# Three of four block sums of x by accumulating transfers, with their casts and splits in new places

## The reference

```
q = cond @ Wq.T + bq                       # one row per batch, 16 heads of 32
k = x @ Wk.T + bk
v = x @ Wv.T + bv
scores = einsum over the 32 values of a head of q / sqrt(32) and k
attn = clip(scores, 0, 1)                  # one number per row and head
context = attn * v                         # per head
out = x + context @ Wo.T + bo
```

## Time and profile before

| what | value |
|---|---|
| three timed runs | 187.72, 187.91, 188.17 us (median 187.91) |
| the profiled execution's own time | 188.1 us |
| its span, first to last instruction | 186.3 us |
| PE busy | 182.5 us, 98% of the span |
| DVE busy | 168.8 us, 91% |
| ACT busy | 115.4 us, 62% |
| POOL busy | 14.7 us, 8% |
| granted PE clock | 1.00 of full speed (2.4 GHz) throughout |
| transfers | 28.09 MB, 151 GB/s over the span |
| the chain of work that ended last | PE 96%, DMA 2% |

### The profile page before, as it was taken

How to read it: one execution, slowest core, us unless ns; L and a number is a source line. 1 busy time by engine, 2 the same in 40 slices (tenths; PEclk the granted TensorE clock), 3 DMA queues, 4 the chain that set the end, 5 groups by cost and what they waited for, 6 DMA issues and landing times.

```text
span 186.3 us, 2377 instructions
## 1 busy us (share of the span) xinstructions
PE 182.5 (98%) x811; PEld 149.1 (80%) x811; DVE 168.8 (91%) x186; ACT 115.4 (62%) x158; POOL 14.7 (8%) x21
## 2 busy tenths in 40 slices
PE   8999999999999999999999999999999999999993
PEld 2788878878878888888888888888888888888883
DVE  0799998999999999999999999998997899799763
ACT  3589873977469685745388574862686574775200
POOL 8000000000000010021000010111000010111000
PEclk9999999999999999999999999999999999999999
DMA  5999910006600006289992006299920007289795
GB/s 218 340 388 425 408 62 2 0 0 193 253 10 0 0 0 116 113 126 230 246 421 106 0 0 116 113 134 296 246 115 0 0 0 116 113 127 279 157 369 194
DMA packets 8075, 28.09 MB, mean 151 GB/s; under 512 B 897, under 2 KB 1281, under 8 KB 7937
## 3 DMA queue, kind: packets, MB, share of 16 engines
q1 hardware_dynamic: 6336, 21.67, 30.4%
q0 software_dynamic: 1728, 6.29, 19.9%
HBM read 19.57 MB, written 8.39 MB: 150 GB/s over the span
## 4 chain that ended last, share of the span: by engine, by line
PE 96%; DMA 2%; ACT 0%; DVE 0%; issue 0%
PE bank_y L337 9%; PE bank_y L341 9%; PE bank_y L339 9%; PE bank_x L337 8%; PE bank_x L341 8%; PE bank_x L339 8%; PE bank_z L341 6%; PE bank_z L339 6%; PE bank_z L337 6%; PE bank_x L415 4%; PE score_bank L397 4%; PE score_bank L396 4%; PE bank_z L415 3%; PE bank_x L433 2%; DMA work<-first_t 2%; PE bank_y L415 1%
## 5 line engine op out<-in xcount | busy, mean ns | idle before, releaser
L574 ACT CAST form_hi<-work 128x1024 fp32r<-128x1024 f32 x28 | 29.0, 1051 | 24.6 <-PE score_bank L397 11.5
L850 DVE TENSOR_TENSOR form_lo<-work,form_hi 128x1024 fp32r<-128x1024 f32 (+1 forms) x38 | 40.2, 1077 | 4.3 <-ACT form_hi L574 4.3
L609 ACT ACTIVATE work<-bank_y,const 128x512 f32<-128x512 f32 x30 | 19.9, 688 | 9.6 <-PE bank_y L341 9.6
L831 POOL DMA_DIRECT2D work<-x_t x12 | 10.5, 875 | 150.7 <-DVE work L885 144.4
L337 PE MATMUL bank_x<-form_hi,wo_hi 128*128 128x512 f32 x52 | 20.3, 390 | 0.0
L339 PE MATMUL bank_x<-form_lo,wo_hi 128*128 128x512 f32 x52 | 20.2, 389 | 0.0
L341 PE MATMUL bank_x<-form_hi,wo_lo 128*128 128x512 f32 x52 | 20.2, 389 | 0.0
L609 ACT ACTIVATE work<-bank_x,const 128x512 f32<-128x512 f32 x24 | 16.0, 686 | 5.3 <-PE bank_x L341 5.3
L874 DVE SCALAR_TENSOR_TENSOR work<-relu,work 128x1024 f32<-128x1024 f32 x16 | 19.1, 1217 | 0.0
L337 PE MATMUL bank_y<-form_hi,wv_hi 128*128 128x512 f32 x48 | 18.8, 391 | 0.0
L341 PE MATMUL bank_y<-form_hi,wv_lo 128*128 128x512 f32 x48 | 18.7, 389 | 0.0
(11 more groups left out here) (153 smaller groups left out, 393.9 us busy)
## 6 DMA issues: line engine op xcount, KB each, us to landing
x_raw<-x_t SPq DMA_DIRECT2D x16, 512.0 KB, 7.0
out_t<-work SPq DMA_DIRECT2D x14, 512.0 KB, 3.3
work<-x_t POOLq DMA_DIRECT2D x12, 512.0 KB, 5.6
work<-first_t SPq DMA_DIRECT2D x2, 512.0 KB, 3.8
work<-wq_t SPq DMA_DIRECT2D x2, 512.0 KB, 8.7
work<-wk_t SPq DMA_DIRECT2D x2, 512.0 KB, 11.2
work<-wo_t SPq DMA_DIRECT2D x1, 1024.0 KB, 13.6
out_t<-work SPq DMA_DIRECT2D x3, 256.0 KB, 2.0
```

Source lines behind the costliest of these rows:

```text
L574: nc.scalar.copy(flat(form_hi, kind), raw(kind, phase)).then_inc(hi_ready[kind], 1)
L609: nc.scalar.activation(result_set(phase)[:, q, j * ROWS:(j + 1) * ROWS], of[:, j, :], ACT.Identity, bias=bias[:, tile:tile + 1], scale=sca ...
L831: pool.dma_start(output_set(s)[:, q, :], x_t[s, q], accum_op=ALU.add).then_inc(residual_added[q], 16)
L850: return nc.vector.tensor_tensor(to, of, hi.bitcast(F32), ALU.subtract)
```

## The change

The four x sums of each super-chunk were four DVE instructions. Now only T1 is one. T3, T2 and T4 are made by transfers that POOL issues and that add a block of x from HBM onto what lies in SBUF: T3 adds Q22 onto Q12 in `x_raw`, T2 adds Q22 onto T1 in `x_sum`, T4 adds Q21 onto T2 in `x_sum`. A transfer of T2 waits until T1 is both cast and split, one of T4 until T2 is both cast and split. In POOL's list these nine transfers stand between the twelve residual transfers. `next_x` waits for T1 of the super-chunk before instead of the split of T4.

Then the lists of ACT and DVE are written in another order. `hi(T4, 1)` now stands directly ahead of `copy_u2(1)`; `hi(T4, 3)` and `hi(T4, 5)` now stand behind `copy_u2(3)` and `copy_u2(5)`, where they stood ahead. The splits `lo(T4, ...)` move accordingly. In the opening, several copies and casts of weights change places.

```diff
@@ sync
             def next_x(s):
                 if s > 1:
-                    sp.wait_ge(lo_ready[T4], made(T4, VALUES_AT[s - 1]))
+                    sp.wait_ge(x_t1_ready, s - 1)
@@ scalar, order of the steps (cut)
             first_hi(T3, Q12)
-            wv_sum_part(S4, 2)
+            first_values(Q11, banks[0], 0)
             first_hi(B22, Q22)
-            first_values(Q11, banks[0], 0)
-            first_values(Q21, banks[1], 2)
...
             first_values(Q22, banks[0], 6)
             hi(B11, 1)
             hi(B21, 1)
             round_scores(0, 0)
-            hi(T4, 1)
-            wo_sum_part(S4, 3)
+            hi(T2, 1)
             hi(T3, 1)
             round_scores(0, 1)
             hi(B22, 1)
             copy_b11(1)
             relu_scores(0, 0)
             relu_scores(0, 1)
+            hi(T4, 1)
             copy_u2(1)
             hi(B11, 2)
...
-            hi(T4, 3)
             hi(B22, 3)
             hi(B11, 4)
             round_scores(2, 0)
+            hi(B21, 4)
             copy_u2(3)
-            hi(B21, 4)
+            hi(T4, 3)
             hi(T1, 4)
+            relu_scores(2, 0)
             copy_u3(3)
@@ gpsimd
-            for s in range(3):
-                at = OUTPUTS_AT[s]
-                add_residual(s, Q11, out11_added, at)
-                add_residual(s, Q22, out22_added, at)
-                add_residual(s, Q21, out21_copied, 2 * at)
-                add_residual(s, Q12, out12_added, at)
+            def x_t3(s):
+                pool.wait_ge(x_t1_ready, s)
+                pool.dma_start(x_raw[:, Q12, :], x_t[s, Q22], accum_op=ALU.add).then_inc(x_t3_ready, 16)
+
+            def x_t2(s):
+                pool.wait_ge(hi_ready[T1], made(T1, VALUES_AT[s]))
+                pool.wait_ge(lo_ready[T1], made(T1, VALUES_AT[s]))
+                pool.dma_start(x_sum[:, :], x_t[s, Q22], accum_op=ALU.add).then_inc(x_t2_ready, 16)
+
+            def x_t4(s):
+                pool.wait_ge(hi_ready[T2], made(T2, VALUES_AT[s]))
+                pool.wait_ge(lo_ready[T2], made(T2, VALUES_AT[s]))
+                pool.dma_start(x_sum[:, :], x_t[s, Q21], accum_op=ALU.add).then_inc(x_t4_ready, 16)
+
+            x_t3(1)
+            x_t2(1)
+            x_t4(1)
+            for s in range(2):
+                residual_11(s)
+                x_t3(s + 2)
+                x_t2(s + 2)
+                residual_22(s)
+                x_t4(s + 2)
+                residual_21(s)
+                residual_12(s)
@@ vector, the three sums go
-            def x_t3(phase):
-            def x_t2(phase):
-            def x_t4(phase):
@@ vector, order of the steps (cut)
             lo(B11, 1)
             lo(B21, 1)
             split_scores(0, 0)
-            lo(T4, 1)
+            wo_sum_part(S3, 2)
+            lo(T2, 1)
             lo(T3, 1)
+            lo(B22, 1)
             split_scores(0, 1)
-            lo(B22, 1)
             context(0, Q11)
             context(0, Q21)
-            wo_sum_part(S3, 2)
             add_out11(1)
             context(0, Q12)
+            lo(T4, 1)
             context(0, Q22)
             lo(B11, 2)
```

More of the change, by code:

```diff
@@ L801, in _ @@
             copy_u2(5)
+            hi(T4, 5)
             hi(T1, 6)
@@ L838, in _, with residual_11, residual_22, residual_21 @@
             nc.gpsimd.tensor_copy(select[:, :], const[:, C_SELECT:C_SELECT + P]).then_inc(select_ready, 1)
-            for s in range(3):
-                at = OUTPUTS_AT[s]
-                add_residual(s, Q11, out11_added, at)
-                add_residual(s, Q22, out22_added, at)
-                add_residual(s, Q21, out21_copied, 2 * at)
-                add_residual(s, Q12, out12_added, at)
+            def residual_11(s):
+                add_residual(s, Q11, out11_added, OUTPUTS_AT[s])
+            def residual_22(s):
+                add_residual(s, Q22, out22_added, OUTPUTS_AT[s])
+            def residual_21(s):
+                add_residual(s, Q21, out21_copied, 2 * OUTPUTS_AT[s])
+            def residual_12(s):
+                add_residual(s, Q12, out12_added, OUTPUTS_AT[s])
+            def x_t3(s):
[20 more added lines that the diff above has]
+                residual_12(s)
+            residual_11(2)
+            residual_22(2)
+            residual_21(2)
+            residual_12(2)
         @block.vector
@@ L934, in x_t1 @@
                 dve.wait_ge(x_loaded[Q12], loads(Q12, s))
+                if s > 1:
+                    dve.wait_ge(hi_ready[T4], made(T4, VALUES_AT[s - 1]))
                 nc.vector.tensor_tensor(x_sum[:, :], x_raw[:, Q11, :], x_raw[:, Q12, :], ALU.add).then_inc(x_t1_ready, 1)
-            def x_t3(phase):
[L939 to L942, removed]
-            def x_t2(phase):
[L946 to L949, removed]
-                nc.vector.tensor_tensor(x_sum[:, :], x_sum[:, :], x_raw[:, Q22, :], ALU.add).then_inc(x_t2_ready, 1)
-            def x_t4(phase):
-                s = PHASES[phase][1]
-                dve.wait_ge(hi_ready[T2], made(T2, phase))
-                dve.wait_ge(x_t2_ready, s)
-                dve.wait_ge(x_loaded[Q21], loads(Q21, s))
-                nc.vector.tensor_tensor(x_sum[:, :], x_sum[:, :], x_raw[:, Q21, :], ALU.add).then_inc(x_t4_ready, 1)
             def add_x(q):
@@ L1191, in _ @@
             add_out12(1)
+            lo(T3, 2)
+            split_scores(1, 1)
             context_t4(2)
-            split_scores(1, 1)
-            lo(T3, 2)
             add_out11(2)
+            x_t1(3)
             lo(T4, 2)
             lo(B22, 2)
-            x_t1(3)
             lo(B21, 3)
-            split_a(1)
-            x_t3(3)
+            context(1, Q11)
             lo(T1, 3)
-            x_t2(3)
+            context(1, Q12)
             add_out22(2)
-            lo(T2, 3)
-            lo(T3, 3)
-            context(1, Q11)
-            x_t4(3)
-            context(1, Q12)
-            add_out12(2)
-            lo(T4, 3)
-            add_out11(3)
-            lo(B22, 3)
-            split_scores(2, 0)
-            lo(B11, 4)
-            context_t1(4)
             context(1, Q21)
             context(1, Q22)
+            lo(T3, 3)
+            lo(T2, 3)
+            add_out12(2)
+            lo(B22, 3)
+            add_out11(3)
+            lo(B11, 4)
+            split_scores(2, 0)
+            context_t1(4)
             lo(B21, 4)
+            context_t3(4)
+            lo(T4, 3)
             lo(T1, 4)
@@ L1223, in _ @@
             lo(T2, 4)
-            context_t3(4)
+            context_t4(4)
             lo(B11, 5)
-            context_t4(4)
             x_t1(5)
+            context(2, Q11)
+            lo(T4, 4)
             add_out12(3)
-            lo(T4, 4)
+            lo(T3, 4)
             split_scores(2, 1)
-            lo(T3, 4)
+            lo(B22, 4)
             add_out11(4)
-            lo(B22, 4)
             lo(B21, 5)
-            x_t3(5)
-            context(2, Q11)
+            context(2, Q21)
             context(2, Q12)
+            context(2, Q22)
             lo(T1, 5)
-            x_t2(5)
             add_out22(4)
@@ L1242, in _ @@
             lo(T2, 5)
-            x_t4(5)
-            context(2, Q21)
-            context(2, Q22)
-            lo(T4, 5)
             add_out12(4)
```

64 lines of the change are left out of this document (31 added, 33 removed).

## The result

The change makes the kernel slower: 190.72 us median of four runs (190.30, 190.42, 191.02, 192.12) against 187.90 of four, a ratio of 1.0162 with a 95% interval from 1.0106 to 1.0218. The forecast was 188.8, in a range up to 190.1. The profiled execution took 190.42 us with a span of 188.6, 2.3 us more than before.

A forecast was written before the change was run, and what follows sets the result against it. PE's never-empty matmul queue was taken as the bound, so only new PE waits count: one wait of 0.85 us on the profiled 188.1 gives 188.95, and with the runs' median 0.2 lower, 188.8 us; range 187.7 to 190.1.

The forecast's parts named there:

- What bounds the kernel: From 5 to 183 us PE's matmul queue never runs dry; waits sum to 0.2 us, any new wait adds in full.
- the lighter DVE would give nothing: Some 11 us of DVE sums removed beside PE's work: worth 0; the rival that it gives something, 187.6 at best, had 0.03.
- PE's rows before 50 us moved by more than 0.2 us: One of the signs named in advance that would show the forecast wrong.
- Super-chunk 1: T4 issued at 41.4, landing at 48.7 after 7.3 us, delays U2's copy; PE starts T3 of phase 1 0.85 us late.
- The prediction's other estimate, 6.7: Landing of T4 in super-chunk 1 if transfer and loads took turns: 5.5 plus 1.2 us; 0.25 us of wait.
- Super-chunks 2 and 3: Phases 3 and 5: T4's transfer issued at 83.3 lands by 91.9, cast and split by 94.1; cost 0.
- 4 us of slack: Super-chunk 2: T4 cast and split by 94.1 at the latest, against PE's need at 98.14.
- The bound of 8.6: Longest landing of the twelve residual transfers before, beside a load and two stores; taken as upper limit for T4's landing.
- PE's need of T4 at 98.14: Phase 3: the time PE needs T4, taken as the deadline for its cast and split.
- another wait, in phases 2 to 5, by a residual or by T2 that lands late: Rival: such a wait costs 0.5 to 1.5 us, time 188.4 to 189.4 if it comes alone; chance 0.06.

The follow-up runs named there:

- e4: Changed kernel with only the old wait put back: the next super-chunk's loads wait for T4's split; 187.95 us, ratio 0.9996.
- e9: The kernel of e4 run again for its profile at full clock; 187.64 us, ratio 0.9986.
- e13: The kernel of e9 once more, timed in more rounds (12 runs); 187.57 us, ratio 0.9984.
- e12: Changed kernel with the moves of e3 and e7 together; 189.55 us, ratio 1.0083.
- e11: Changed kernel with the old wait on T4's split put back for the loads of super-chunk 3 alone; 188.35 us, ratio 1.0030.
- e2: Changed kernel with the sum T2 back on DVE, T3 and T4 still transfers; 188.49 us, ratio 1.0044.
- e7: Changed kernel with ACT's casts of T4 behind the copies of U3 in phases 3 and 5, DVE's splits one place later; 189.37 us, ratio 1.0072.
- e3: Changed kernel with T4's cast in phase 1 behind the copy of U2 and the score rounding, its split behind the score split; 191.53 us, ratio 1.0156.
- e10: Changed kernel with the old wait on T4's split put back for the loads of super-chunk 2 alone; 188.72 us, ratio 1.0037.
- e1: Changed kernel with the sum T4 back on DVE, T3 and T2 still transfers; 188.54 us, ratio 1.0039.

## Why the prediction was wrong

**What bounds the kernel: right.** PE has no slack, and every pause went into the span in full: 3.1 us of pauses, less 0.8 of a shorter opening, is 2.3 us. That the lighter DVE would give nothing was right too, within what can be told; e4, e9 and e13, which have all of the change but the loads' wait, lie 0.04% to 0.16% below the kernel before. One of the prediction's own signs of being wrong, PE's rows before 50 us moved by more than 0.2 us, came with the 0.8 of the opening; executions of the kernel before have spans from 185.6 to 186.6, so that much of it may be scatter.

**Super-chunk 1: right in place and cause; the size is close in part by luck.** T4's transfer was issued at 41.02 (forecast 41.4) and took 6.6 us (forecast 7.3), the cast started at 47.66 (48.7), and PE paused 0.68 us (0.85). Two errors worked against each other. The landing was 0.7 us shorter than forecast, but the issue came only 8.3 us ahead of PE's T3 (49.35), where the forecast had 8.8 (41.4 and 50.16): PE came 0.8 us earlier, the issue only 0.4. Beside the same loads it took 6.6 in e12, 6.8 in e11, 6.9 in e2 and e7, 7.1 in e3; without them 5.3 to 5.5 in e9, e10 and e13. So a meeting with three loads costs 1.1 to 1.8 us. The prediction's other estimate, 6.7, which is 5.5 alone and the 1.2 of one load, is nearer to this than the 7.3 taken. It goes with what the Trainium skill says of turns between queues packet by packet (DMA: Bandwidth & Descriptors, section Queues, rings and completion order), and here the trace roughly agrees. In super-chunk 2 it doesn't: four loads cost 3.3 us (9.2 against 5.9 in e13), not 1.2.

**Super-chunks 2 and 3: the step that failed.** The prediction put it: "T2's cast now follows the copies ... transfer issued at 83.3, landing at 88.8 (5.5) to 91.9 (8.6) ... 4 us of slack. Cost 0." Three things were wrong in it.

1. T2's own landing stood nowhere in the sum; its cast was put at 80.8, behind the copies. It took 7.7 us and landed at 83.6. The transfer of T4 waits for T2's cast and split, so it was issued 3.2 us later than forecast, at 86.49. e9, with a landing of 5.5, shows 83.99, so 2.5 of the 3.2 go with the late landing.
2. So T4's transfer came upon the four loads of super-chunk 3, which started at 86.54 as before and which the loosened wait no longer held back, and took 9.2 us. The bound of 8.6, the longest of the twelve before, wasn't one. e13 puts a price on the loads alone: issued as late, T4 takes 5.9, so 3.3 us are theirs.
3. The deadline was read at the wrong instruction. The prediction compared with PE's need of T4 at 98.14. But behind the cast in ACT's list stand the cast of T1 of phase 4, a `relu` and the copy of U3, and PE needs that copy first. Counted back from there: 0.1 for the signal, 1.25 for the copy, 2.5 for the three starts ahead of it (95.67 to 98.15), 3.85 in all, gives 94.3. In the profiled execution PE would have come to T4 at 97.9 (99.46 less 1.55), so the deadline was 94.05. T4 landed at 95.7, 1.6 us too late: the measured pause.

With the right deadline and the latest forecast landing, 91.9, there would still have been 2.4 us of slack. It took the late T2 and the loads together, and that shows in the table above: e13 has the first alone and e2 the second alone, and neither waits there. The method that found the first wait, counting back from ACT's list, was simply not applied a second time, and landings were bounded by single transfers of a kernel with 12 accumulating ones, where now there are 21. The rival closest to the event, "another wait, in phases 2 to 5, by a residual or by T2 that lands late", had 0.06 of the chance.

**The third wait**, near 141, has one load beside it (at 130.01 us) and not four, since there is no super-chunk 4. T4's transfer of super-chunk 3 took 8.2 to 8.9 us in the nine profiles beside e4's that have it, in e13 too, which doesn't wait. By the same count the cast of T4 must start 3.85 us ahead of PE's first matmul of T4. In the change it started at 138.62, 3.2 ahead of where PE would have come (142.41 less 0.64, 141.77): 0.7 too late, which is about the pause. In e10, e13 and e3 it started 3.9, 3.8 and 3.8 ahead (138.02 and 141.94; 136.27 and 140.07; 140.75 and 144.55), and there is no wait. So all of them stand on the edge. The setback of DVE by the wait near 98 isn't enough for an explanation: in e10 DVE stood idle there for 2.3 us and PE paused 1.97, longer than in the change (2.2 and 1.66), and the third wait didn't come. What e10 has less is landing, 7.0 against 7.4 for T2 and 8.2 against 8.6 for T4. A few tenths of a landing thus decide, and why they differ is open.

**The scatter** of the changed kernel, 190.30 to 192.12, was not settled. A stretch at half clock as in e3 is not it: the two slowest, 191.02 and 192.12, have a mean granted clock of 1.000. Which wait grows in them can't be seen, since only the one of 190.42 was profiled.

## What to carry to other kernels

Where a change puts a transfer into a chain of dependent steps, look for what will run beside it, and for the waits that kept it apart. Here a semaphore wait, loosened because the data allowed it, would have held four loads back until T4 was through; putting that one line back gave all of some 2.8 us. The loads needn't have moved for this: those of super-chunk 3 stayed where they were, and the transfer came to them. Compute the slack of a landing at every place where it recurs, and at the first instruction that is needed behind the waiting one in its engine's list, not only at the consumer of the data. And don't judge a landing by how full the DMA engines are, neither by the mean of 0.64 nor in the few microseconds of the transfer: from 88 to 92 us they are as full in e13 (0.98 and 1.06) as in the change (1.00 and 0.91), and T4 lands after 5.9 us in one and 9.2 in the other. What counts is which transfers share them.

## What the runs showed of the hardware

- An accumulating transfer of 512 KB took 5.3 to 5.5 us to land with little beside it (T4 of super-chunk 1 in e9, e10 and e13), and 6.6 to 7.1 beside three plain loads of the same size. With two more accumulating ones behind it in its queue it took 5.9 to 6.1 without loads (T4 of super-chunk 2 in e9, e11, e13), 9.2 to 9.6 beside four that started with it (the change, e3, e7, e10, e12), and 7.4 beside four of which the first started 1 us later (e2).
- T2's transfer in super-chunk 2, issued between 75.64 and 76.02 us in seven kernels, landed after 5.5, 5.7, 5.9 (e9, e11, e1) or 7.4, 7.6, 7.7, 7.7 (e13, e7, the change, e10). How full the DMA engines were from 76 to 84 us doesn't part the two: 0.85, 0.92, 1.00 in the first group, 0.91, 0.90, 0.93, 0.94 in the second. What decides is open.
- A pause of PE of 2.28 us in a queue that was dense otherwise was followed, after 1.3 us of matmuls, by some 3.3 us at half clock (e3's profile); after the pause of 1.97 us in e10's profile (189.85 us) the clock stayed at 1.00. That is one execution each.
